# Layer 1's first deviation ahead of later gathers, idle products in the first tiles, another order for the maxima, and layer 0's clearing on GpSimd

## The chip, the core and the metric

## The reference

Two layers over x of 4 x 1024 rows of 256, with a context of 77 rows per batch. Each layer is cross-attention with 16 heads of 16 and then a feed-forward part: eight experts, two per row, in layer 0, and a low-rank one in layer 1.

```python
x = x + xattn0(_layernorm(x), ctx, ctx)       # Q = q@Wq ..., causal, softmax(Q K^T) V @ Wp
x = x + experts(_layernorm(x))                # router, top 2 of 8, gelu(x w1) w2, weighted sum
# layer 1's attention, the part that most of the change is in:
v = einsum('nlhd,ed->nlhe', v, Wv); k = einsum('nlhd,ed->nlhe', k, Wk); q = einsum('nlhd,ed->nlhe', q, Wq)
energy = einsum('nqhd,nkhd->nhqk', q, k)
attention = softmax(energy / sqrt(256), axis=-1)
x = x + (einsum('nhql,nlhd->nqhd', attention, v).reshape(N, Lq, 256) @ Wo.T + bo)
x = x + lowrank_ffn(_layernorm(x))            # gelu(x U1 V1 + b1) U2 V2 + b2
```

## The kernel before

The 4096 rows are 32 tiles of 128 (NT = 32), a group is four tiles. The order of every engine's instructions is written out by hand, as loops over steps k in each engine's block; `wait_ge` and `after` (the same, left out for values up to zero) are the waits. The stages follow one another with a barrier between them: preparation, `attend_first` (layer 0's attention), `route`, `experts`, `attend` (layer 1's attention) and `feed_forward`. Instructions of small helpers carry the helper's line.

**Layer 0's attention.** Step k turns the rows of tile k + 5 (L770), makes the queries of tile k + 4 (L778), which ScalarE scales into `qhi` (L828) and DVE into the low part (L899), and works on scores, exponentials and heads of earlier tiles. ScalarE copies the turned rows into `xT` (L866). GpSimd makes the reciprocal deviation `rstd` of tile k + 5 from DVE's variance (L656, L658), copies the high part into `qcat` twice (L631) and builds the block-diagonal keys `bd` (L623). Before the first step DVE clears `qcat` and `v_ps` (L892, L893), and ScalarE waits for `v_ok`, which the second of them sets, before all else.

**Layer 1's attention.** For tile f, two indirect DMAs on GpSimd's queue gather the experts' results `y1`, `y2` (L1583) while SP loads x; DVE adds them up and takes mean and variance (L1818 to L1828, the row work); GpSimd makes `rstd` and `shift` (L1600, L1603), and, one tile later, adds the bias `bo` to X (L1591); ScalarE norms the rows (L1757), PE turns them (L1705), ScalarE keeps the high f16 part (L1751) and DVE the low part (L1833). PE multiplies the high part with the keys, four products of four heads (`scores`, L1641), and DVE takes the maxima. For the first five tiles (EARLY) the four products go to the four banks of `sT_ps` and one instruction takes all maxima (L1844). For later tiles they share one bank, `s_ps`, so that each waits for the maximum before it (L1838). The maxima of a group are scaled by DVE (`mcat`, L1852), turned by PE (`maxima_transposed`, L1648) and copied by ScalarE to `mT` (L1784). Their place is `mT_ps`, in the bank `v_ps`, that also takes the values' products (L1679) and the turned heads (`heads_out`, L1632).

Then the scores are made again by key (`scores_by_key`, L1667) in four terms, the last of which subtracts the maxima; ScalarE takes exponentials (L1763), PE multiplies by the values, ScalarE copies out, PE turns the heads back, DVE divides by the sums (`heads`, L1859 and L1862), PE turns the result (L1690) and projects it (L1697) into the first half of `pr_bank`, and DVE adds it to X (`result`, L1868). Step k does this for quarter k, while its later part belongs to tile n = k - 5 and its earlier part to tile f = k + 5. Steps 5 to 26 have both and are called full here; a boundary is the passage from one group to the next. DVE's order in a full step is low part, heads, first and second maximum, row work of tile f + 2, third maximum, result, fourth maximum. PE's is heads, first scores, scores by key, second scores, and so on.

The experts' stage has idle products already, `awake` (L1328): products whose result nobody reads.

## Time and profile before

| | us |
|---|---|
| three runs, median (lowest to highest) | 1058.36 (1057.31 to 1061.56) |
| the profiled execution | 1060.01 |
| its span | 1058.0 |
| PE, DVE, ACT, POOL busy in it | 910.3, 621.1, 512.5, 423.3 |
| layer 0's attention begins, first work on PE | 36.4 |
| layer 1's attention, first gather to last result | 732.9 to 958.5 |

The profile records one execution. Its busy shares are means over stages with different limits, so they say little alone; the timeline gives, for each instruction or run of like ones, the start from the span's beginning, the time it took, and in brackets how long its engine had been idle and what ended that. A time "high" or "low" of the clock is the granted clock of 1.00 or 0.50.

### The profile page before, as it was taken

The page shows a single profiled execution, that of the slowest core. Times are in us where ns is not written, and L with a number is a line of the kernel's source. Part 1 is how long each engine was busy: PE and PEld are TensorE (multiplying, and loading weights), DVE is VectorE, ACT ScalarE, POOL GpSimd, SP SyncE. Part 2 cuts the span into 40 slices and gives each one's busy share as a digit, 9 for nine tenths or more (in the row PEclk, how much of TensorE's full clock was granted, in tenths as well). Part 3 has the DMA queues.
Part 4 walks back from the last instruction along what each step waited for, and adds up shares of the span by engine and source line. Part 5 has one row for each costly group of instructions (what it writes and reads, how often), then busy time and mean ns, then how long its engine had stood idle before and what let it go on. Part 6 is the DMA issues. An engine that isn't in the chain of part 4 may idle for free. (4 is left out here: it accounts for less than half of the span.)

```text
span 1058.0 us, 23850 instructions
## 1 busy us (share of the span) xinstructions
PE 910.3 (86%) x7874; PEld 627.0 (59%) x7874; DVE 621.1 (59%) x1484; ACT 512.5 (48%) x865; POOL 423.3 (40%) x592
## 2 busy tenths in 40 slices
PE   5799999997027999999999999995479888879996
PEld 3445656554016889898988989874124444445552
DVE  4567888876795444454444444322768888645561
ACT  1478888875311333323333333342266666645663
POOL 2377777762102423333221222212865665104451
PEclk9789999999557999999999999998568999999999
DMA  6323444334420111112111121112324222000212
GB/s 181 72 77 99 137 125 133 111 102 148 163 79 20 54 49 45 57 41 61 41 49 53 42 61 41 51 46 70 100 70 112 67 71 56 1 1 5 54 45 61
DMA packets 73727, 75.42 MB, mean 71 GB/s; under 512 B 22730, under 2 KB 66874, under 8 KB 73626
## 3 DMA queue, kind: packets, MB, share of 16 engines
q1 hardware_dynamic: 67146, 56.31, 17.9%
q0 software_dynamic: 6480, 17.70, 6.5%
q8 instruction: 71, 1.16, 0.5%
q14 instruction: 30, 0.25, 0.1%
HBM read 51.64 MB, written 22.34 MB: 70 GB/s over the span
## 5 line engine op out<-in xcount | busy, mean ns | idle before, releaser
L1496 DVE CAST hh_e<-h_e 128x512 f16<-128x512 f32 x128 | 59.4, 464 | 178.1 <-ACT h_e L1446 105.3
L1347 PE MATMUL up_ps<-xT_e,experts 128*128 128x256 f16 x512 | 139.6, 273 | 0.7 <-DVE xT_e L1488 0.6
L1361 PE MATMUL y_ps<-experts,hh_e 128*128 x512 | 139.6, 273 | 0.0
L1362 PE MATMUL y_ps<-experts,hh_e 128*128 x512 | 139.6, 273 | 0.0
L1348 PE MATMUL up_ps<-xT_e,experts 128*128 128x256 f16 x512 | 139.6, 273 | 0.0
L1363 PE MATMUL y_ps<-experts,hh_e 128*128 x512 | 139.6, 273 | 0.0
L1349 PE MATMUL up_ps<-xT_e,experts 128*128 128x256 f16 x512 | 139.6, 273 | 0.0
L1273 POOL COPY idx_e<-token 128x2 int32 (+2 forms) x39 | 22.5, 577 | 286.4 <-PE xT_ps_e L1322 237.0
L1446 ACT ACTIVATE h_e<-up_ps 128x512 f32<-128x512 f32 x128 | 76.4, 597 | 87.5 <-PE up_ps L1349 87.5
L1498 DVE TENSOR_TENSOR hh_e<-h_e,hh_e 128x512 f16<-128x512 f32 x128 | 88.6, 692 | 4.4
L1763 ACT ACTIVATE prob_a<-sT_ps_a 77x1024 f32<-77x1024 f32 x64 | 64.9, 1015 | 42.1 <-PE sT_ps_a L1667 42.1
L1276 POOL DMA_INDIRECT x_e<-xh_scratch,idx_e x71 | 69.5, 979 | 36.6 <-POOL idx_e L1273 26.9
L1583 POOL DMA_INDIRECT y_a<-y_scratch,slots_t x64 | 63.2, 987 | 36.9 <-POOLq L1266 21.6
L623 POOL TENSOR_TENSOR experts<-keys,blocks 128x616 f16<-128x616 f16 x64 | 76.5, 1216 | 0.0
L1439 ACT ACTIVATE xT_e<-xT_ps_e 128x512 f16<-128x512 f32 (+1 forms) x39 | 21.8, 558 | 100.2 <-PE xT_ps_e L1322 100.2
L820 ACT ACTIVATE experts<-sT_ps 77x1024 f32<-77x1024 f32 x64 | 65.1, 1018 | 8.4 <-PE sT_ps L692 5.4
L1838 DVE TENSOR_REDUCE nmax_a<-s_ps_a 128x4 f32<-128x308 f32 x108 | 51.2, 474 | 23.8 <-PE s_ps_a L1641 22.3
L2116 ACT ACTIVATE h_f<-h_ps_f,b_f 128x512 f32<-128x512 f32 x64 | 43.1, 687 | 30.2 <-PE h_ps_f L2058 30.2
L913 DVE TENSOR_REDUCE qcat<-s_ps 128x8 f16<-128x616 f32 x64 | 51.1, 798 | 8.7 <-PE s_ps L718 4.6
L1347 PEld LDWEIGHTS up_ps<-xT_e,experts 128*128 x512 | 50.1, 98 | 7.1 <-issue 1.2
L1362 PEld LDWEIGHTS y_ps<-experts,hh_e 128*128 128x128 f16 x512 | 50.1, 98 | 6.0
L1349 PEld LDWEIGHTS up_ps<-xT_e,experts 128*128 x512 | 50.1, 98 | 5.9
(328 smaller groups left out, 2115.0 us busy)
## 6 DMA issues: line engine op xcount, KB each, us to landing
experts<-in_L_ffn_w SPq DMA_DIRECT2D x22, 512.0 KB, 4.1
y_scratch<-y_e SPq DMA_DIRECT2D x32, 256.0 KB, 3.4
x<-in_x SPq DMA_DIRECT2D x32, 128.0 KB, 3.3
experts<-in_x SPq DMA_DIRECT2D x64, 64.0 KB, 2.5
x_scratch<-x SPq DMA_DIRECT2D x16, 256.0 KB, 2.5
xh_scratch<-xn SPq DMA_DIRECT2D x16, 256.0 KB, 2.8
w_r<-in_L_ffn_w SPq DMA_DIRECT2D x8, 512.0 KB, 4.3
x_a<-x_scratch SPq DMA_DIRECT2D x32, 128.0 KB, 2.6
```

The source lines that it names most:

```text
L623: nc.gpsimd.tensor_tensor(bd[:, f % 2, flat(i, 2), :, :], G["khi"][0][:, b, heads].rearrange("p (q k) -> p q k", q=2)[:, :, None, :] .broa ...
L820: nc.scalar.activation(prob[:, k % 2, qh, :, :], sT_ps[0:KEYS, :, :], ACT.Exp).then_inc(exp_ok, 1)
L1276: pool.indirect_dma_start(out=x[:, n, :], out_offset=None, in_=A["xh"], in_offset=bass.IndirectOffsetOnAxis(ap=idx[:, n:n + 1], axis=0)) \
L1347: mm(out, w[0], xT[0][:, c, 0:W_], start=c == 0, stop=False)
L1348: mm(out, w[0], xT[1][:, c, 0:W_], start=False, stop=False)
L1349: last = mm(out, w[1], xT[0][:, c, 0:W_], start=False, stop=c == DC - 1)
L1361: mm(out, a[0], w[0], start=m == 0, stop=False)
L1362: mm(out, a[0], w[1], start=False, stop=False)
L1363: last = mm(out, a[1], w[0], start=False, stop=m == 7)
L1446: nc.scalar.activation(h[:, q % 2, 0:2 * width(k)], up_ps[q][:, 0:2 * width(k)], ACT.Gelu, scale=1 / WSCALE).then_inc(gelu_ok, 1)
L1498: nc.vector.tensor_tensor(hh[1][own], h[own], hh[0][own], ALU.subtract).then_inc(hlo_ok, 1)
L1763: nc.scalar.activation(prob[:, k % 2, 2 * half:2 * half + 2, :], sT_ps[0:KEYS, 2 * half:2 * half + 2, :], ACT.Exp, scale=1.0 / 16).then_in ...
```

## The change

Layer 0: GpSimd clears `qcat` ahead of its steps, the low part of tile 0 waits for it (`qcat_ok`), and ScalarE's wait for `v_ok` goes. Six groups of six idle products are put between PE's first instructions. Layer 1: GpSimd's gather for tile f + 1 instead of f + 3 stands ahead of tile f's deviation, with two tiles gathered ahead of the loop and none in its first pass; the bias is added eight tiles later. PE does 52 idle products ahead of the first rows and two and six around each early tile's scores. `mT_ps` moves to the second half of `pr_bank`, with the waits that go with it. The second scores of a step are issued ahead of the last term of the scores by key, and DVE takes the first maximum between the reciprocal of the sums and the heads' product.

```diff
@@ attend_first, GpSimd
+                nc.gpsimd.memset(qcat[:, :, :, :], 0.0).then_inc(qcat_ok, 1)
+                pool.wait_ge(qcat_ok, 1)
                 for k in STEPS:
                     f = k + 3
                     if tile(k + 4):
-                        if k == -4:
-                            pool.wait_ge(v_ok, 1)
                         high_twice(k + 4)
@@ attend_first, PE
+                def awake(count):
+                    for i in range(count):
+                        mm(sT_ps[:, 0, 0:D], G["ident16"][:, :], G["khi"][0][:, 0, 0:D], start=True, stop=True)
                 for k in STEPS:
                     if tile(k + 4):
                         queries(k + 4, k)
+                    if k in (-4, -3):
+                        awake(6)
                     if tile(k + 3):
                         high_transposed(k + 3, k)
...
                         rows_transposed(k + 5, k)
+                    if k in (-5, -4, -3, -2):
+                        awake(6)
@@ attend_first, ACT and DVE
-                act.wait_ge(v_ok, 1)
-                nc.vector.memset(qcat[:, :, :, :], 0.0)
                 nc.vector.memset(v_ps[:, :], 0.0).then_inc(v_ok, 1)
...
+                    if f == 0:
+                        dve.wait_ge(qcat_ok, 1)
@@ attend
-        mT_ps = v_ps[:, 0:D].bitcast(F16)
+        mT_ps = pr_bank[:, D:2 * D].bitcast(F16)
@@ attend, GpSimd
-                for f in range(3):
+                LAG = 8
+                for f in range(2):
                     gather(f)
                 pool.wait_ge(bo_in, 16)
                 for f in range(NT):
-                    if f + 3 < NT:
-                        gather(f + 3)
+                    if f and f + 1 < NT:
+                        gather(f + 1)
...
-                    if f > 0:
-                        biased(f - 1)
-                biased(NT - 1)
+                    if f >= LAG:
+                        biased(f - LAG)
+                for f in range(NT - LAG, NT):
+                    biased(f)
@@ attend, PE
-                    pe.wait_ge(mT_ok, min(k // 4 + 1, GROUPS))
...
                 def maxima_transposed(g):
                     pe.wait_ge(mc_ok, g + 1)
-                    after(pe, oe_ok, 4 * g - 1)
+                    after(pe, mT_ok, g)
+                    after(pe, x3_ok, 4 * g - 5)
...
                 def scores_by_key(k):
-                    pe.wait_ge(mT_ok, g + 1)
                     for term in range(4):
+                        if term == 3:
+                            pe.wait_ge(mT_ok, g + 1)
+                            if tile(k + 5) and k + 5 not in EARLY:
+                                scores(k + 5, 1)
...
                 def projection(n):
+                    pe.wait_ge(mT_ok, min((n + 5) // 4 + 1, GROUPS))
...
+                awake(52)
                 for k in STEPS:
                     if f in EARLY:
+                        awake(2)
                         for i in range(4):
                             scores(f, i)
+                        awake(6)
...
                         scores_by_key(k)
-                    if late:
-                        scores(f, 1)
@@ attend, DVE
+                def sums(n):
+                    dve.wait_ge(o_done, n + 1)
+                    nc.vector.reciprocal(rec[:, n % 2, :], heads_bank(n)...[:, :, HD]).then_inc(rec_ok, 1)
...
                     if tile(n):
-                        heads(n)
+                        sums(n)
                     if late:
                         maximum(f, 0)
+                    if tile(n):
+                        heads(n)
+                    if late:
                         maximum(f, 1)
```

GpSimd's queue at the start of layer 1's attention, before (the gathers are the DMAs of y_a, `rstd_a` is the deviation, `X<-X,bo_a` the bias):

```order
L1583 DMA y_a<-y_scratch,slots_t 128x256 x6
L1583 DMA y_a<-y_scratch,slots_t 128x256 [waits bo_in_a]
L1583 DMA y_a<-y_scratch,slots_t 128x256
L1600 TENSOR_TENSOR rstd_a<-ve_a,neghalf 128x1 [waits var_ok_a]
L1603 TENSOR_SCALAR shift_a<-mv_a,rstd_a 128x1 [waits rstd_ok_a]
L1583 DMA y_a<-y_scratch,slots_t 128x256 [waits x2_ok_a]
L1583 DMA y_a<-y_scratch,slots_t 128x256
L1600 TENSOR_TENSOR rstd_a<-ve_a,neghalf 128x1 [waits var_ok_a]
L1603 TENSOR_SCALAR shift_a<-mv_a,rstd_a 128x1 [waits rstd_ok_a]
L1591 TENSOR_TENSOR X<-X,bo_a 128x256 [waits xh_ok_a]
```

and now:

```order
L1592 DMA y_a<-y_scratch,slots_t 128x256 x4
L1610 TENSOR_TENSOR rstd_a<-ve_a,neghalf 128x1 [waits var_ok_a,bo_in_a]
L1613 TENSOR_SCALAR shift_a<-mv_a,rstd_a 128x1 [waits rstd_ok_a]
L1592 DMA y_a<-y_scratch,slots_t 128x256 x2
L1610 TENSOR_TENSOR rstd_a<-ve_a,neghalf 128x1 [waits var_ok_a]
L1613 TENSOR_SCALAR shift_a<-mv_a,rstd_a 128x1 [waits rstd_ok_a]
```

Four gathers stand ahead of the first deviation instead of eight, and the bias has left these rows.

PE's queue at a group's boundary in layer 1's attention, with the beginning of the next step, before (`s_ps_a` are scores, `sT_ps_a` the scores by key, `v_ps_a<-const,oTu_a` the heads, `mcat_a` the maxima):

```order
L1641 MATMUL s_ps_a<-keys,xhi_a 128x308 [waits max_ok_a]
L1648 MATMUL v_ps_a<-ident,mcat_a 128x128 [waits oe_ok_a,mc_ok_a]
L1648 MATMUL v_ps_a<-ident,mcat_a 128x128 x3
L1632 MATMUL v_ps_a<-const,oTu_a 128x128 [waits mT_ok_a,oe_ok_a]
L1632 MATMUL v_ps_a<-const,oTu_a 128x128 x3
L1641 MATMUL s_ps_a<-keys,xhi_a 128x308 [waits max_ok_a,hi_ok_a]
L1667 MATMUL sT_ps_a<-xhi_a,keys 77x512 [waits exp_ok_a,lo_ok_a,mT_ok_a]
L1667 MATMUL sT_ps_a<-xhi_a,keys 77x512 x3
L1667 MATMUL sT_ps_a<-xlo_a,keys 77x512 x4
L1667 MATMUL sT_ps_a<-xhi_a,keys 77x512 x4
L1667 MATMUL sT_ps_a<-mT_a,mrows 77x512 x4
L1641 MATMUL s_ps_a<-keys,xhi_a 128x308 [waits max_ok_a]
```

and now:

```order
L1651 MATMUL s_ps_a<-keys,xhi_a 128x308 [waits max_ok_a]
L1660 MATMUL pr_ps_a<-ident,mcat_a 128x128 [waits x3_ok_a,mT_ok_a,mc_ok_a]
L1660 MATMUL pr_ps_a<-ident,mcat_a 128x128 x3
L1642 MATMUL v_ps_a<-const,oTu_a 128x128 [waits oe_ok_a]
L1642 MATMUL v_ps_a<-const,oTu_a 128x128 x3
L1651 MATMUL s_ps_a<-keys,xhi_a 128x308 [waits max_ok_a,hi_ok_a]
L1682 MATMUL sT_ps_a<-xhi_a,keys 77x512 [waits exp_ok_a,lo_ok_a]
L1682 MATMUL sT_ps_a<-xhi_a,keys 77x512 x3
L1682 MATMUL sT_ps_a<-xlo_a,keys 77x512 x4
L1682 MATMUL sT_ps_a<-xhi_a,keys 77x512 x4
L1651 MATMUL s_ps_a<-keys,xhi_a 128x308 [waits max_ok_a,mT_ok_a]
L1682 MATMUL sT_ps_a<-mT_a,mrows 77x512 x4
```

The wait for the eviction has moved from the heads to the last term, a wait for DVE's result has come ahead of the turned maxima, and the second scores have changed places with the last term.

DVE's queue in a full step, before (`nmax_a` the maxima, `o_a` the heads' product, `xa_a` the row work's first instruction):

```order
L1859 RECIPROCAL rec_a<-v_ps_a 128x16 [waits o_done_a]
L1862 TENSOR_TENSOR o_a<-v_ps_a,rec_a 128x256 [waits oT_done_a,rec_ok_a]
L1838 TENSOR_REDUCE nmax_a<-s_ps_a 128x4 [waits s_done_a] x2
L1818 SCALAR_TENSOR_TENSOR xa_a<-y_a,cw_t,x_a 128x256 [waits x_in1_a,y_in1_a]
L1821 SCALAR_TENSOR_TENSOR X<-y_a,cw_t,xa_a 128x256 [waits xa_ok_a]
```

and now:

```order
L1880 RECIPROCAL rec_a<-v_ps_a 128x16 [waits o_done_a]
L1860 TENSOR_REDUCE nmax_a<-s_ps_a 128x4 [waits s_done_a]
L1887 TENSOR_TENSOR o_a<-v_ps_a,rec_a 128x256 [waits oT_done_a,rec_ok_a]
L1860 TENSOR_REDUCE nmax_a<-s_ps_a 128x4 [waits s_done_a]
L1840 SCALAR_TENSOR_TENSOR xa_a<-y_a,cw_t,x_a 128x256 [waits x_in1_a,y_in1_a]
```

The heads' product stands between the first two maxima.

## Rows read from the trace of the kernel before

**Rows 1.** Stretches: us, busy (instructions) by engine, PEclk (granted clock), DMA share, GB/s

```profile
740.00:760.00 20.00, 7.59 (x24) 2.88 (x24) 13.41 (x28) 4.47 (x9) 16.92 (x25) 0.50 0.36 102
...
784.00:788.00 4.00, 4.00 (x26) 0.85 (x25) 2.29 (x7) 1.02 (x2) 2.04 (x3) 0.50 0.24 68
...
820.00:860.00 40.00, 34.63 (x291) 17.69 (x290) 34.05 (x95) 27.32 (x45) 25.55 (x38) 1.00 0.25 71
```

**Rows 2.** Timeline, layer 0's start and one memset before it: start, us, engine, instruction

```profile
8.39 0.95 POOL L259 MEMSET experts<- 128x1024 f16 x1
...
36.82 1.76 DVE L892 MEMSET qcat<- 128x2048 uint32 x1 [0.78 <-PEq L223]
...
39.21 0.38 ACT L866 ACTIVATE experts<-t_ps 128x256 f32<-128x256 f32 x1 [3.42 <-DVE v_ps L893]
...
40.09 0.57 POOL L658 TENSOR_TENSOR rstd<-ve,neghalf 128x1 f32<-128x1 f32 x1
...
41.81 0.47 ACT L828 ACTIVATE experts<-q_ps,rstd 128x256 f16<-128x256 f32 x1 [1.27 <-PE q_ps L778]
...
54.50 0.47 ACT L828 ACTIVATE experts<-q_ps,rstd 128x256 f16<-128x256 f32 x1 [1.97 <-POOL rstd L658]
```

**Rows 3.** Timeline, layer 1's first tiles, and the gathers' own view, last row

```profile
734.16 0.95 POOL L1583 DMA_INDIRECT y_a<-y_scratch,slots_t  x1 [0.30 <-issue]
...
737.66 0.48 DVE L1818 SCALAR_TENSOR_TENSOR xa_a<-y_a,cw_t,x_a 128x256 f32<-128x256 f32 x1 [4.47 <-DMA y_a<-y_scratch,slots_t]
...
739.38 0.15 DVE L1828 TENSOR_SCALAR ve_a<-mv_a 128x1 f32<-128x1 f32 x1
...
742.73 0.59 POOL L1600 TENSOR_TENSOR rstd_a<-ve_a,neghalf 128x1 f32<-128x1 f32 x1
...
746.17 0.58 POOL L1600 TENSOR_TENSOR rstd_a<-ve_a,neghalf 128x1 f32<-128x1 f32 x1
...
746.87 1.44 DVE L1844 TENSOR_REDUCE nmax_a<-sT_ps_a 128x16 f32<-128x1232 f32 x1 [0.92 <-PE sT_ps_a L1641]
...
747.08 0.72 POOL L1591 TENSOR_TENSOR X<-X,bo_a 128x256 f32<-128x256 f32 x1
...
747.96 1.03 POOL L1583 DMA_INDIRECT y_a<-y_scratch,slots_t  x1 [0.17 <-issue]
...
750.28 0.58 POOL L1600 TENSOR_TENSOR rstd_a<-ve_a,neghalf 128x1 f32<-128x1 f32 x1
...
DMA to landing us min/median/max: 2.7/2.8/4.4
```

**Rows 4.** Timeline, a full step, and the result of a group earlier or later

```profile
841.88 0.41 DVE L1868 TENSOR_TENSOR X<-pr_ps_a,X 128x256 f32<-128x256 f32 x1
...
843.71 0.47 DVE L1838 TENSOR_REDUCE nmax_a<-s_ps_a 128x4 f32<-128x308 f32 x1
...
844.24 0.30 PE L1641 MATMUL s_ps_a<-keys,xhi_a 128*128 128x308 f16 x1
...
844.58 0.48 DVE L1838 TENSOR_REDUCE nmax_a<-s_ps_a 128x4 f32<-128x308 f32 x1 [0.40 <-PE s_ps_a L1641]
...
847.14 0.41 DVE L1868 TENSOR_TENSOR X<-pr_ps_a,X 128x256 f32<-128x256 f32 x1
...
864.33 0.41 DVE L1868 TENSOR_TENSOR X<-pr_ps_a,X 128x256 f32<-128x256 f32 x1
```

**Rows 5.** Waits from 804 to 910 us: who for whom, us, times, longest

```profile
DVE nmax_a L1838 <- PE s_ps_a L1641: 7.6, 19, 0.4
...
DVE rec_a L1859 <- PE v_ps_a L1632: 4.1, 5, 0.8
```

**Rows 6.** Timeline of PE: the experts' idle products

```profile
326.69 5.30 PE L1328 MATMUL up_ps<-experts,ident 128*128 128x256 f16 x24 [3.69 <-PEq L1061]
```

**Rows 7.** Timeline, exponentials of the first and the sixth step

```profile
769.61 1.93 ACT L1763 ACTIVATE prob_a<-sT_ps_a 77x1024 f32<-77x1024 f32 x2
...
799.30 1.02 ACT L1763 ACTIVATE prob_a<-sT_ps_a 77x1024 f32<-77x1024 f32 x1 [2.07 <-PE sT_ps_a L1667]
```

17 lines of the change are left out of this document (11 added, 6 removed).

## The prediction

> **What bounds the kernel now.** I read the busy shares by stage first [rows 1]. Layer 1's attention, from 732 us on, is the stage that most of the change touches. From 740 to 760 us TensorE (PE) is busy 7.59 of 20 us, at a granted clock of 0.50 (1.2 of 2.4 GHz), and GpSimd 16.92 of 20 us. So its first tiles hang on GpSimd; the timelines show that the steps after them hang on PE and DVE in turn.
>
> *Layer 0's start* [rows 2]: DVE clears qcat (1.76 us) and then v_ps; ScalarE waits 3.42 us for that and makes xT of tile 0 only at 39.21; the queries follow, and qhi of tile 0 comes at 41.81. Its reciprocal deviation was ready at 40.09 + 0.57 = 40.66. Three tiles on, the same ScalarE instruction waits for GpSimd instead (1.97 us at 54.50), and GpSimd's own loop sets the pace.
>
> *Layer 1's start* [rows 3]: tile 0's variance is ready at 739.38 + 0.15 = 739.53 (its data came at 737.66), but GpSimd has eight indirect gathers of about 1.25 us each ahead of its deviation, which starts at 742.73. Then GpSimd is full: two gathers, deviation, shift and bias addition make 4.11 us per tile (746.17 to 750.28).
>
> *A full step at the high clock* [rows 4], one of about 20: the first maximum (843.71) ends at 844.18; TensorE can only then overwrite s_ps (844.24), and the second maximum starts at 844.58. DVE waits 0.40 us, and this wait is there 19 times between 804 and 910 us, 7.6 us in all [rows 5]. DVE has no other wait of that size in a plain step. The step is 5.26 us (the result's starts, 841.88 and 847.14). *At a group's boundary* PE waits for ScalarE to evict the maxima from v_ps, and DVE then up to 0.8 us for the heads behind it: 4.1 us in five boundaries [rows 5]. Four steps with one boundary take 864.33 - 841.88 = 22.45 us [rows 4]. That is 4 x 5.26 = 21.04 and 1.41 more: about 0.5 us for DVE's scaling of the maxima, an instruction as long as a maximum's 0.47, and 0.9 for the boundary.
>
> **The change part by part.** All is summed against the profiled execution, 1060.01 us (span 1058.0); it lies 1.65 us above the median of the three runs, 1058.36.
>
> *1. Layer 0's start.* v_ok no longer holds ScalarE: xT of tile 0 can start at about 36.9, and its queries end near 38.6. But qcat is now cleared on GpSimd, ahead of tile 0's deviation on the same queue, as 4096 elements of two bytes. GpSimd's memset of 1024 such took 0.95 us [rows 2]: four times that is 3.8 us, and a little less, 3.5, since an instruction's fixed part is paid once. From 36.8 that is 40.3, then about 0.4 us to the deviation and 0.57 for it: it is ready at 41.3, 0.65 us later than now, and qhi of tile 0 starts at about 41.35 instead of 41.81: **-0.45 us**. What was the late input (the queries) is early, and the deviation is late next. The 36 idle products lie in these steps too; 24 such products took 5.30 us at the low clock [rows 6], 0.21 us each with 0.2 for the last one's latency, and at the high clock it would be 0.11. Twelve of them stand between one tile's queries and the next tile's in the third step: 2.6 us low, 1.3 high. At the high clock a tile's own queries would take about 1 us less. With GpSimd next in line (54.50) most of either is hidden. Bounds: -1.5 us (one tile's queries gained) to +2.2 (2.6 us paid, 0.45 kept).
>
> The Trainium skill says in "VectorE: DVE Perf Modes", section on zero memsets as uint32, that a memset costs one cycle per element whatever the type, so that clearing by four bytes halves it. It speaks against this move: with GpSimd's 1.2 GHz (the Trainium skill, "GPSIMD Engine Reference", Specifications) 4096 elements would be 3.4 us, an estimate, against the 2048 words that DVE cleared. GpSimd's own row agrees with it, and term 1 would be -0.55 us by it.
>
> *2. Layer 1's first deviation.* Four gathers stand ahead of it instead of eight. They end at about 737.6, so it waits only for the variance and starts at 739.6 instead of 742.73: **-3.1 us** for tile 0. Tile 1's follows the next two gathers, at 743.0 instead of 746.17, the same.
>
> *3. The first tiles after it.* The bias addition (0.72 us, 0.88 with its gap: 747.08 to 747.96) leaves GpSimd's loop for eight tiles: 4.11 - 0.88 = 3.23 us. DVE is next: low part, early maxima (1.44 us) and row work need 0.4 + 1.4 + 1.9 = 3.7 us (the row work from 737.66 to 739.53), and a gather now runs only one tile ahead, landing 2.8 us after its issue in the median and about 3.5 at the first (734.16 to 737.66) [rows 3]. Walking the chain tile by tile gives 3.7 to 4.0 us, seven tiles of 0.1 to 0.4 less, minus a hold-up at tile 2 of up to 0.4. I take **-1.2 us** (bounds -0.6 to -1.9). The bias additions return from tile 8 on in GpSimd's idle time (1 to 2 us a step) and the last eight run at its end, where nothing is due soon.
>
> *4. 92 idle products in layer 1.* Fifty-two stand ahead of the first transposes. The 24 from 326.69 on ran at the low clock to the end [rows 6]; the 52 go on for twice as long. If half of the 52 run at 0.21 and half at 0.11 us, they end near 740.6, and the first transposes are due at 741.3: nothing. All at the low clock, they end at 743.3: +2.0. The eight per tile (1.7 us low, 0.9 high) fit into PE's idle time (12.4 of 20 us [rows 1], five tiles: 2.5 us each). Gain: the five steps from the first exponentials (769.61) to the sixth step's (799.30) take 29.7 us now [rows 7], 5.9 each, mostly at 0.50. At the high clock a maximum, its turn through PE and the next maximum are 0.87 us apart (843.71 to 844.58), 0.93 to 0.97 with what lies between; three of these, 0.4 and the row work of 1.8 make 5.0 us a step, and with one scaling of the maxima 25.5 us: -4.2. At the low clock PE is full, 6.6 us a step at most; the second scores go ahead of a quarter of the score work, 0.4 us earlier: 6.2 a step, 31 us: +1.3. No products stand in these steps, and from 784 us on the clock was at 0.50 although PE was busy 4.00 of 4 us [rows 1]. So I take mostly low: **-1.2 us** (bounds -4.2 to +2.8, the latter with one step with heads at the low clock, 1.5 us more).
>
> *5. Maxima reordered.* In a full step DVE now does low part, reciprocal, first maximum, head product, second maximum; PE issues the second scores ahead of the last term. With [rows 4]: the first maximum can start at 843.37 and ends at 843.84; scores at 843.95, 0.30 us; second maximum at 844.30 instead of 844.58: 0.28 saved of the 0.40. But two more chains then lie at about 5.0 us: PE's own (0.28 us of its small gaps, about 0.45 a step, go) and the projection, that waits on exponentials which now start after the second scores. I take 0.23: 21 steps (the sixth to the 26th, as the loops count them) x 0.23 = **-4.8 us** (0 to -8.4).
>
> *6. Maxima through pr_bank.* PE need no longer wait for the eviction before the heads. But the transposes now wait for the result that DVE reads from that bank (847.14 + 0.41, behind the third maximum), and then stand ahead of the heads: about 0.2 us of wait is left of 0.9, so 0.7 at each of six boundaries with heads: **-4.2 us** (-2 to -5.5).
>
> Sum: -0.45 - 3.1 - 1.2 - 1.2 - 4.8 - 4.2 = **-14.95 us**, or 1045.1 for the profiled execution and **1043 us** for a median (1058.36 - 14.95 = 1043.4). The last stage starts earlier by the whole of it, since it waits for this one only.
>
> **The rivals.** (a) *The clock stays high through the first steps.* The sum's term 4 becomes -4.2: 1040 us. For it: steps with heads, little different in kind, run at it. Against: 784 to 788 us [rows 1]. [...] (b) *The reordering moves the wait.* The exponentials come later behind the second scores, PE's queue with them, and the step stays at 5.26: without term 5, 1048 us. (c) *The products are paid at the low clock*: term 1 at +2.2, term 4 at +2.8: 1043.4 + 2.65 + 4.0 = 1050. (d) *Slower: the clock stays low in the steps with heads.* A step at the low clock takes some 6 us without heads; heads, their transposes and the projection add about 2 us there: 8 against 5.0, 3 us more a step. It decides from the fifth such step on (15 us), from the seventh by over 0.5%; ten make 1043 + 30 = 1073 us. Against it: with heads the clock is at 1.00 and PE busy 34.63 of 40 us from 820 on [rows 1], and shorter waits leave PE busier, not idler. (e) *The first deviation is not what holds the first tiles*, since gathers landing late take its place: term 2 halved and term 3 at zero, 1046 us, within the forecast's range.
>
> **How the numbers follow.** Forecast with (e) 0.55; (a) 0.18; (b) 0.12; (c) 0.12; (d) 0.03. The range from 1035 (a with terms 5 and 6 at their better bounds, in part) to 1051 (c) leaves about 2 in 10 out. A measurement of this kernel tells 0.5%, 5.3 us, from no change: faster by more needs less than 1053, which all but (d) and the end of (c) give: 0.92; within 0.5%: 0.05; slower: 0.03.
>
> **What would show it.** Tile 0's deviation at 3 us before its old place, from the stage's start; early maxima 3.7 to 4.0 us apart; the wait of 0.40 us ahead of the second maximum below 0.15 and full steps of 5.0 us; four steps with a boundary in about 20.8 us; no wait of PE for the eviction. In layer 0 qhi of tile 0 within half a microsecond of now, behind GpSimd's clearing of 3.5 us. The granted clock from 741 to 800 us tells (a) from the forecast. The prediction is wrong if full steps stay at 5.26 us, or if the products stand ahead of transposes that are ready.

## The result, and the profile after

| | us |
|---|---|
| before, seven runs | 1059.04 (1054.92 to 1061.56) |
| changed, seven runs | 1051.73 (1046.83 to 1058.75) |
| ratio, 95% interval | 0.9937 (0.991 to 0.9964) |
| changed, the profiled execution (span) | 1047.91 (1045.8) |
| changed, all 19 executions, later ones included | 1049.65 (1040.53 to 1059.79) |

The change gains 7.3 us in the first seven runs and 9.4 over all its executions; the forecast had 15 to 16. The changed kernel's 19 executions lie 19 us apart, those of the kernel before 4 to 9 in each group of runs. A ratio leaves out executions over 1.5% above the fastest of their kernel, which here touches one only, the 1059.79 of e5.

Among the first seven runs the time goes with the mean granted clock: 1046.8 and 1047.9 us at 0.945, 1057.6 and 1058.8 at 0.932 and 0.933. The profiled execution is the second fastest of them and 3.8 us below their median, so its trace shows more gain than the median does.

Where the 12.2 us between the two profiled executions lie, with two later profiles of the same changed kernel (e5, e17) beside them:

| stretch | before | changed | e5 | e17 | forecast of the difference |
|---|---|---|---|---|---|
| layer 0: DVE's first clearing to `qhi` of tile 0 | 4.99 | 4.42 | 4.42 | 4.43 | -0.45 |
| layer 0: DVE's first clearing to the router's logits | 242.67 | 240.21 | 240.28 | 248.60 | the same -0.45 |
| layer 1: `mcat` cleared to the copy-out of quarter 0 | 44.25 | 39.86 | 39.79 | 39.84 | -4.3 (terms 2, 3) |
| copy-outs 0 to 5 (steps 0 to 4) | 29.58 | 31.25 | 29.99 | 25.34 | -1.2 (term 4) |
| copy-outs 5 to 26 (full steps) | 116.17 | 110.96 | 111.02 | 109.75 | -8.3 (term 5, five boundaries of term 6) |
| copy-out 26 to the last result | 36.14 | 34.60 | 35.96 | 34.61 | -0.7 (the sixth boundary) |

Each interval runs from start to start; DVE's first clearing is that of `qcat` in the kernel before (36.82) and that of `v_ps` in the changed one (36.48). The rows add up to 11.9 us; the other 0.3 lie elsewhere.

The timeline of the changed kernel at both starts (answers to [rows 2], [rows 3] and, for idle products, [rows 6]):

```profile
36.29 3.52 POOL L642 MEMSET qcat<- 128x4096 f16 x1 [21.65 <-POOLq L223]
36.48 0.48 DVE L900 MEMSET v_ps<- 128x512 f32 x1 [0.47 <-PEq L223]
40.24 0.57 POOL L658 TENSOR_TENSOR rstd<-ve,neghalf 128x1 f32<-128x1 f32 x1
40.90 0.47 ACT L837 ACTIVATE experts<-q_ps,rstd 128x256 f16<-128x256 f32 x1 [2.80 <-POOL rstd L658]
...
729.28 5.84 PE L1727 MATMUL pr_ps_a<-keys,ident 128*128 128x256 f16 x52 [2.59 <-PEq L1275]
735.07 0.48 DVE L1840 SCALAR_TENSOR_TENSOR xa_a<-y_a,cw_t,x_a 128x256 f32<-128x256 f32 x1 [4.85 <-DMA y_a<-y_scratch,slots_t]
737.11 0.68 POOL L1610 TENSOR_TENSOR rstd_a<-ve_a,neghalf 128x1 f32<-128x1 f32 x1 [2.48 <-DVE ve_a L1850]
741.34 1.44 DVE L1866 TENSOR_REDUCE nmax_a<-sT_ps_a 128x16 f32<-128x1232 f32 x1 [0.92 <-PE sT_ps_a L1651]
744.81 1.43 DVE L1866 TENSOR_REDUCE nmax_a<-sT_ps_a 128x16 f32<-128x1232 f32 x1
```

GpSimd's clearing takes 3.52 us (estimate 3.5), and `qhi` of tile 0 now waits 2.80 us for the deviation behind it. In layer 1 the deviation starts 737.11 - 729.36 = 7.75 us after `mcat` is cleared, where it was 742.73 - 732.33 = 10.40; it waits for DVE's variance now, not for the later gathers ahead of it in its queue. That variance follows tile 0's own data, which landed 735.07 - 729.36 = 5.71 us after the clearing and not 737.66 - 732.33 = 5.33: this later landing takes 0.4 of the 3.1 us that were forecast. The next early maximum follows in 3.47 us. The 52 products took 5.84 us, 0.11 each: all at the high clock, and over (735.12) as DVE's first row work began (735.07).

A full step and the waits from 804 to 910 us (answers to [rows 4] and [rows 5]):

```profile
839.39 0.42 DVE L1893 TENSOR_TENSOR X<-pr_ps_a,X 128x256 f32<-128x256 f32 x1 [0.21 <-PE pr_ps_a L1713]
...
840.69 0.48 DVE L1860 TENSOR_REDUCE nmax_a<-s_ps_a 128x4 f32<-128x308 f32 x1
841.09 0.41 DVE L1887 TENSOR_TENSOR o_a<-v_ps_a,rec_a 128x256 f32<-128x256 f32 x1
841.70 0.48 DVE L1860 TENSOR_REDUCE nmax_a<-s_ps_a 128x4 f32<-128x308 f32 x1 [0.20 <-PE s_ps_a L1651]
...
844.56 0.42 DVE L1893 TENSOR_TENSOR X<-pr_ps_a,X 128x256 f32<-128x256 f32 x1 [0.21 <-PE pr_ps_a L1713]
...
860.88 0.42 DVE L1893 TENSOR_TENSOR X<-pr_ps_a,X 128x256 f32<-128x256 f32 x1 [0.21 <-PE pr_ps_a L1713]
```

```profile
DVE nmax_a L1860 <- PE s_ps_a L1651: 6.5, 20, 1.5
DVE X L1893 <- PE pr_ps_a L1713: 5.7, 20, 0.6
...
DVE rec_a L1880 <- PE v_ps_a L1642: 1.4, 5, 0.3
```

DVE's wait ahead of the second maximum is 0.20 us, half of the 0.40 before. A new wait of 0.21 us stands ahead of the result, for the projection. The boundary's wait ahead of the reciprocal fell from 4.1 to 1.4 us. The step from 839.39 to 844.56 is 5.17 us, and four steps with a boundary take 860.88 - 839.39 = 21.49 (5.26 and 22.45 before).

ScalarE's copy-outs of the quarters 0, 5 and 26, before and then changed, mark the stretches of the table:

```profile
776.58 0.60 ACT L1769 ACTIVATE oTu_a<-v_ps_a 128x512 f32<-128x512 f32 x1 [1.06 <-PE v_ps_a L1679]
806.16 0.60 ACT L1769 ACTIVATE oTu_a<-v_ps_a 128x512 f32<-128x512 f32 x1 [0.21 <-PE v_ps_a L1679]
922.33 0.60 ACT L1769 ACTIVATE oTu_a<-v_ps_a 128x512 f32<-128x512 f32 x1 [0.25 <-PE v_ps_a L1679]
```

```profile
769.22 0.60 ACT L1791 ACTIVATE oTu_a<-v_ps_a 128x512 f32<-128x512 f32 x1 [0.85 <-PE v_ps_a L1694]
775.91 0.60 ACT L1791 ACTIVATE oTu_a<-v_ps_a 128x512 f32<-128x512 f32 x1 [0.85 <-PE v_ps_a L1694]
...
800.47 0.60 ACT L1791 ACTIVATE oTu_a<-v_ps_a 128x512 f32<-128x512 f32 x1
...
911.43 0.60 ACT L1791 ACTIVATE oTu_a<-v_ps_a 128x512 f32<-128x512 f32 x1 [0.30 <-PE v_ps_a L1694]
```

The dense steps 0 to 4 gave 1.7 us back: the first three take 6.69 us each at the low clock (769.22 to 775.91 for one).

Two stretches, columns as in [rows 1], 766 to 792 us for the dense steps:

```profile
740.00:760.00 20.00, 13.08 (x81) 7.88 (x85) 17.08 (x37) 5.51 (x11) 14.68 (x21) 0.84 0.36 102
766.00:792.00 26.00, 23.85 (x128) 6.83 (x124) 15.95 (x43) 13.71 (x21) 13.96 (x20) 0.50 0.31 80
```

The clock was at 0.84 in the early tiles (0.50 before) and at 0.50 in the dense steps, with PE busy 23.85 of 26 us.

Three questions follow. What are the idle products worth, and do they make the executions differ? Why do terms 5 and 6 bring 5.2 us instead of 8.3 in the full steps? What sets the clock in steps 0 to 4?

### The profile page after: what moved, and what is told of

Its sections match the earlier page's. It is cut to its first block and busy times, and to the rows that moved or that the text cites. A ratio compares the mean times of both kernels' runs of the same rounds, so it can differ in the third digit from the quotient of the medians.

```text
span 1045.8 us, 24107 instructions
## 1 busy us (share of the span) xinstructions
PE 920.9 (88%) x8002; PEld 636.3 (61%) x8002; DVE 612.4 (59%) x1483; ACT 510.1 (49%) x865; POOL 426.8 (41%) x593
## 5 line engine op out<-in xcount | busy, mean ns | idle before, releaser
L1505 DVE CAST hh_e<-h_e 128x512 f16<-128x512 f32 x128 | 55.3, 432 | 183.1 <-ACT h_e L1455 118.8
```

## Experiments

Every kernel computes all of the reference. "Changed" is the kernel after the change.

| run | kernel | median (lowest to highest), runs | ratio to before, interval |
|---|---|---|---|
| e1 | changed, no products in layer 1 | 1046.58 (1044.22 to 1050.58), 5 | 0.9871 (0.9845 to 0.9897) |
| e2 | changed, no products in layer 0 | 1046.95 (1042.76 to 1049.82), 6 | 0.9888 (0.9863 to 0.9913) |
| e3 | changed, order of maxima as before | 1050.08 (1047.84 to 1057.09), 7 | 0.9922 (0.9894 to 0.995) |
| e4 | before, order of maxima alone | 1055.77 (1047.94 to 1060.52), 12 | 0.997 (0.9946 to 0.9993) |
| e5 | changed again | 1047.79 (1040.53 to 1059.79), 6 | 0.9886 (0.9847 to 0.9925) |
| e6 | changed, no products at all | 1047.05 (1046.37 to 1048.09), 6 | 0.9891 (0.9869 to 0.9913) |
| e7 | before, gathers alone | 1056.63 (1052.55 to 1059.91), 12 | 0.9975 (0.9957 to 0.9994) |
| e8 | changed, more products in steps 0 to 4 | 1044.68 (1042.19 to 1057.69), 6 | 0.9899 (0.9854 to 0.9944) |
| e9 | e8 without layer 0's products | 1041.98 (1039.29 to 1044.52), 5 | 0.9842 (0.9817 to 0.9868) |
| e10 | products in steps 0 to 4 alone | 1041.29 (1038.75 to 1045.67), 6 | 0.9841 (0.9816 to 0.9866) |
| e11 | before, products alone | 1057.49 (1055.51 to 1062.27), 12 | 0.9999 (0.9979 to 1.0019) |
| e12 | before, maxima's bank alone | 1055.60 (1051.15 to 1058.10), 12 | 0.9962 (0.9944 to 0.998) |
| e13 | e10 with layer 0's products | 1042.86 (1041.61 to 1045.41), 5 | 0.9856 (0.9837 to 0.9874) |
| e14 | e10 again | 1045.15 (1044.47 to 1047.24), 4 | 0.9879 (0.9861 to 0.9897) |
| e15 | e10, second scores between halves | 1045.57 (1043.27 to 1046.99), 4 | 0.9875 (0.9855 to 0.9895) |
| e16 | before, products in steps 0 to 4 | 1064.06 (1060.39 to 1065.75), 6 | 1.005 (1.0033 to 1.0067) |
| e17 | changed, third time | 1049.56 (1044.46 to 1050.77), 6 | 0.9902 (0.9875 to 0.993) |
| e18 | e10, third time | 1040.41 (1039.01 to 1043.88), 5 | 0.9838 (0.9812 to 0.9865) |

### The products taken away: e1, e2, e6, and alone: e11

e1 takes this out:

```diff
-                awake(52)
...
-                        awake(2)
...
-                        awake(6)
```

> The changed kernel without the idle products of layer 1 (52, and eight per early tile). The changed kernel ran at 1051.7 us in the median, spread over 12 us, where the one before spread over 6.6. Theory 1: the products give a high clock from about 742 to 756 us and nothing after; the early tiles go by DVE and GpSimd, so without the products the time is 0 to 1.5 us longer (1052 to 1053) and the spread stays. Theory 2: the products are what makes the executions differ, since work done ahead of the dense steps moves the low stretch of the clock into them: without them the median falls to 1047 to 1049 and the spread to 7 us or less, and the first five dense steps take 29.7 us or less instead of 31.0.

e2 takes out layer 0's two:

```diff
-                    if k in (-4, -3):
-                        awake(6)
...
-                    if k in (-5, -4, -3, -2):
-                        awake(6)
```

> The changed kernel without the 36 idle products of layer 0. In its profile the clock was high from 46 us on where it had been low to 56 us before, and the route stage began 2.8 us earlier. Theory 1: all of that but the earlier deviation (0.9 us) comes from the products: without them the median is 1.5 to 2 us longer, about 1053.5, and the clock is low from 40 to 55 us again. Theory 2: it comes from ScalarE's earlier start and GpSimd's loop, and the products are idle cost: the median stays within 0.5 us of 1051.7, and the route stage still begins within 0.5 us of 276.7.

e6 takes out all four.

> The changed kernel without any of its idle products, in layer 0 as in layer 1. Theory 1 (products neither gain nor cost): 1047 us like each half, groups of 21.1 us, the first five dense steps 29.5 to 31.3. Theory 2 (each half's products cost about 5 us in the median): 1042 to 1044. Theory 3 (the products gain, and the two kernels without half of them drew well): 1050 or more, with the clock low from 40 to 55 us.

e11 is the kernel before with the same four places filled.

> The kernel before with only the idle products of both layers, placed as in the change. Theory 1 (they gain 0.4 us in layer 0 and nothing in layer 1, and widen the spread): a median of 1057 to 1060 us, executions from 1050 to 1066. Theory 2 (they gain what the forecast gave them, 1 to 3 us): 1056 to 1058, spread 6 us. In either, the clock is high through the early tiles of layer 1, where GpSimd sets the pace, so that no time is gained there.

Without the products of either layer the time does not rise. It is 1046.6, 1047.0 and 1047.1 us in e1, e2 and e6, against 1049.65 over the changed kernel's 19 executions, and e6's six executions lie within 1.7 us. Beside e6, though, the changed kernel itself (e5) ran at 1047.8 with a ratio of 0.9886, where e6 has 0.9891: side by side there is no difference, so that the products cost anything in the median is not shown. In the kernel before the products alone bring nothing (0.9999, give or take 2 us; its median is 1.5 us lower), and its executions lie no further apart there. So the change's gain comes from its other parts. Theory 1 of e1 (up to 1.5 us longer) was wrong; of its theory 2 the lower median held, but e1's first five dense steps took 31.23 us, so the products do not move the low clock into those. Both theories of e2 were wrong (1053.5, and 1051.7 with the next stage at 276.7): it ran at 1047.0, and its logits came at 275.18 us. For e6, theory 1 had the median and the dense steps (31.25) right, but its groups of four steps took 21.5 us and not 21.1. For e11, the median fits both theories, the spread theory 2.

### Where a long execution can lose its time: e17, with e5

e5 and e17 are the changed kernel unaltered.

> The changed kernel itself again, on the chip and beside the kernels of this call. Theory 1 (its executions differ by where the clock is low, and the seven before were a wide draw): a median of 1048 to 1051 us, a profile whose groups of four steps take 21.1 us like those of the two kernels without products (they took 21.5 in most of its first profile). Theory 2 (the products cost): 1051 to 1053 again, 4 us or more above the kernel without any, and groups of 21.5 us.

> The changed kernel a third time. Theory 1 (products ahead of the dense steps in both layers leave room for a long low stretch in layer 0's or layer 1's dense steps in some executions): a median of 1048 to 1052, and one execution or more above 1055. Theory 2 (the calls differ, not the kernels): within 2 us of e18.

The medians were 1047.8 and 1049.6 us, near theory 1's in both; but e5's profile has groups of four steps at 21.5 us (theory 1: 21.1), and e5 had an execution at 1059.79, e17 none above 1050.8 (its theory 1: one above 1055). e17's profile shows where a long one can lose time. Layer 0's stretches 60 to 90 us of the changed kernel, of e17, of e18 and of the kernel before (columns as in [rows 1]):

```profile
60.00:75.00 15.00, 13.53 (x146) 6.88 (x144) 10.62 (x22) 14.01 (x22) 11.84 (x16) 1.00 0.15 43
75.00:90.00 15.00, 13.66 (x154) 7.88 (x151) 8.97 (x22) 13.52 (x23) 10.88 (x16) 1.00 0.46 137
```

```profile
60.00:75.00 15.00, 15.00 (x104) 7.54 (x103) 6.37 (x14) 9.48 (x14) 7.43 (x10) 0.50 0.20 49
75.00:90.00 15.00, 14.78 (x125) 6.97 (x127) 7.50 (x17) 11.54 (x18) 8.98 (x12) 0.67 0.29 89
```

```profile
60.00:75.00 15.00, 13.17 (x152) 7.29 (x152) 10.65 (x22) 14.18 (x23) 11.95 (x15) 1.00 0.16 42
```

```profile
60.00:75.00 15.00, 14.11 (x135) 7.09 (x134) 8.63 (x19) 11.87 (x19) 11.06 (x15) 0.77 0.13 39
```

In e17 PE ran at 0.50 while it was busy 15.00 of 15 us, and did 104 matmuls instead of 146. The router's logits, first of the changed kernel and then of e17, with e17's clearing of `v_ps` ahead:

```profile
276.69 0.49 DVE L1132 TENSOR_TENSOR logits<-logits,lx 128x128 f32<-128x128 f32 x2 [1.53 <-PEq L537]
```

```profile
38.29 0.48 DVE L900 MEMSET v_ps<- 128x512 f32 x1 [0.47 <-PEq L223]
...
286.89 0.49 DVE L1132 TENSOR_TENSOR logits<-logits,lx 128x128 f32<-128x128 f32 x2 [1.52 <-PEq L537]
```

From the clearing they come 276.69 - 36.48 = 240.21 and 286.89 - 38.29 = 248.60 us later: layer 0 took 8.4 us longer with this low stretch. Over all profiles of kernels with GpSimd's clearing the interval is, with layer 0's products, 240.2, 240.3, 240.5, 241.6, 242.3, 243.9 and 248.6 (changed, e5, e8, e13, e1, e3, e17; the clock fell below 1.00 between 60 and 90 us in the last four), and without them 239.2 to 239.7 six times and 242.1 once (e15, 0.77 from 60 to 75). The means are 242.5 and 239.9. Two things lie in that difference of 2.6 us.

The first is there at the high clock too. With the clock at 1.00 from 60 us on, the interval is 240.2 to 240.5 with the products (changed, e5, e8) and 239.2 to 239.7 without (six profiles): they cost 0.8 us, although they bring the early steps, which GpSimd paces, 0.3 to 0.4 us forward (the clock is at 0.97 from 45 to 60 us, 0.61 in e18 without them). In the kernel before it is 241.3 (e11) against 240.4 and 239.9 (e7, e16).

The second is the low stretch between 60 and 90 us, and it comes without layer 0's products as well: in the kernel before itself (0.77 from 60 to 75 us, above), in e4 (0.88), in e12 (0.94) and in e15 (0.77). That makes four of twelve profiles without the products and four of eight with them; the two at 0.50 (e3, e17) both have them. Whether the products bring the low stretch or make it longer is therefore not shown. It also means that the 2.5 us by which the first profile gains in layer 0 are the low stretch in the profile before: e7 and e16, with the old clearing and the clock at 1.00 there, need 240.4 and 239.9 us, not 242.67, and the changed kernel needs 240.2.

e17's dense steps were fast by luck, as the next part shows; an execution with its layer 0 and the first profile's dense steps would be 1049.5 + 31.25 - 25.34 = 1055.4 us, close to the three highest (1057.6 to 1059.8). That those are such executions is inferred from their mean granted clock (0.931 to 0.933, where the profiled ones had 0.945); none of them has a profile.

### The dense steps 0 to 4: e8, e9, e10, e14, e18, e16

e8 adds, behind the last term:

```diff
                     if 0 <= k < QUARTERS:
                         scores_by_key(k)
+                    if 0 <= k < 5:
+                        awake(6)
```

> The changed kernel with six more idle products in each of the steps 0 to 4, behind the last term, where the clock was low from 766 to 793 us. Theory 1 (PE's gaps there keep the clock low): the clock is high from the second of these steps on, and the five steps take 27 us instead of 31.2: 1048. Theory 2 (PE is full at the low clock and the clock comes back by another cause): each product is paid, 6 x 0.21 = 1.26 us a step, 37 us for the five: 1057.

e9 is e8 without layer 0's products, e10 has these products alone.

> The changed kernel without layer 0's idle products, with layer 1's and six more in each of the steps 0 to 4. Theory 1 (the dense steps stay at the high clock when PE's gaps are filled, and layer 0's products bring nothing but a low stretch that falls later): the five steps take 26.6 to 27 us in the profile as in the kernel with all products, the median is 1042.5 to 1044, and no execution lies above 1052. Theory 2 (the far executions come from layer 1's products): the median is about 1044.7 and one in six lies above 1054.

> The changed kernel with no idle products but the six in each of the steps 0 to 4. Theory 1 (products there lift the clock by themselves): the clock, low up to quarter 0, is high from the first or second of these steps on, the five take 27 to 28.5 us instead of 31.25, the median falls from 1047 to 1043.5 or less, and the spread stays at 2 to 3 us. Theory 2 (the clock has to be high before, and at the low clock PE is full, so products are paid): 31.25 + 5 x 1.26 = 37.5 us and a median of 1053.

e14 and e18 repeat e10; e16 puts the products of steps 0 to 4 alone into the kernel before.

> The kernel of e10 again, beside the other three. Both theories: 1040 to 1043 us, steps 0 to 5 in 26.0 us, groups of 21.1 us or with three steps longer by 0.4 us.

> The kernel of e10 and e14 a third time, beside the changed kernel. Theory 1: 1041 to 1045.5 us, 5 us or more below e17, spread 3 to 7 us. Theory 2: within 2 us of e17.

> The kernel before with only six idle products in each of the steps 0 to 4. Theory 1 (the clock stays or turns high once PE's gaps there are filled, whatever the order around): steps 0 to 5 take 26.3 us instead of 29.6, 1055.5 in the median. Theory 2 (the new order of scores is needed for it, since PE's waits at group boundaries and for the maxima are larger here): 29 to 34 us and 1058 to 1063.

The stretches 770 to 790 us of e6, e10 and e16, in this order:

```profile
770.00:780.00 10.00, 8.89 (x52) 2.37 (x56) 5.85 (x16) 4.03 (x8) 5.46 (x7) 0.50 0.21 62
780.00:790.00 10.00, 9.47 (x49) 3.03 (x42) 6.05 (x17) 6.34 (x10) 5.01 (x8) 0.50 0.31 90
```

```profile
770.00:780.00 10.00, 7.95 (x72) 3.19 (x64) 7.44 (x21) 6.23 (x10) 6.44 (x10) 1.00 0.30 81
780.00:790.00 10.00, 9.30 (x80) 4.46 (x79) 8.12 (x23) 7.08 (x13) 6.45 (x10) 1.00 0.75 165
```

```profile
770.00:780.00 10.00, 8.82 (x53) 2.98 (x53) 4.94 (x13) 3.88 (x6) 5.41 (x8) 0.50 0.15 41
```

With 30 products in these steps the clock is high from the first of them on, and copy-outs 0 to 5 take 26.0 us in e9, e10 and e18, 26.6 in e8 and e14, 27.0 in e15 and 28.0 in e13, whose second step takes 6.83 us (both are described below; e6: 31.25). e10, e14 and e18 are 1041.3, 1045.2 and 1040.4 us, and e18 stands 9 us below the changed kernel beside it (e17), the largest gain of the study; e14 fell short of its expectation by 2 us. Theory 1 held for e8, e9, e10 and e18, with times at or below its own, though e10's executions lie 7 us apart and not 2 to 3. e8, which has layer 0's products too, had two executions at 1051.5 and 1057.7 among six. Theory 2, by which PE is full there and each product is paid, is wrong: six take 0.83 us at the high clock (the row is e10's), and the step falls by 1.4 us with them in it (6.69 to 5.30).

```profile
770.89 0.83 PE L1723 MATMUL pr_ps_a<-keys,ident 128*128 128x256 f16 x6
```

But e16, for which theory 2 held, shows that it isn't the products alone: in the kernel before the clock was at 0.50 from 770 to 780 with them, copy-outs 0 to 5 took 30.4 us, and the time rose by 0.5%. Of the 3.1 us that its profile loses from the clearing of `mcat` to copy-out 5, 2.3 lie ahead of copy-out 0 (46.50 us, 44.25 before), where step 0's products stand. And e17 and e4 had the high clock with no product in these steps. Copy-outs 0 and 5 of e17, and copy-out 0 of e4, whose copy-out 5 stands in the next part:

```profile
778.20 0.60 ACT L1791 ACTIVATE oTu_a<-v_ps_a 128x512 f32<-128x512 f32 x1 [0.56 <-PE v_ps_a L1694]
...
803.54 0.60 ACT L1791 ACTIVATE oTu_a<-v_ps_a 128x512 f32<-128x512 f32 x1
```

```profile
778.28 0.60 ACT L1770 ACTIVATE oTu_a<-v_ps_a 128x512 f32<-128x512 f32 x1 [0.85 <-PE v_ps_a L1682]
```

That is 25.34 us, 5.07 a step, in e17, and 26.33 in e4 (clock 0.81 from 780 to 790 us and 1.00 from then on). So the clock was high for most of these steps in all seven profiles that have the products there together with the new order, and in two of the twelve profiles that have no products there. What decides at the end of the early tiles which way the clock goes is open.

### The maxima: e3, e4, e12, e15

e3 puts scores and maxima of the changed kernel back in the old order, e4 puts only the new order into the kernel before, e12 only the new bank and its waits.

```diff
@@ e3 (e4 is the reverse, on the kernel before)
-                        if term == 3:
-                            if tile(k + 5) and k + 5 not in EARLY:
-                                scores(k + 5, 1)
...
+                    if late:
+                        scores(f, 1)
@@ e12
-        mT_ps = v_ps[:, 0:D].bitcast(F16)
+        mT_ps = pr_bank[:, D:2 * D].bitcast(F16)
```

> The changed kernel with the second scores behind the last term again and both maxima behind the heads' product, as before the change; the maxima's bank stays the new one. Theory 1: the reordering is worth what full steps show between the two traces, less the boundaries: 0.1 us in a plain step and 0.4 in one with scaling, so about 3 us: 1054.7, with steps of 5.26 to 5.3 and the wait of 0.4 us ahead of the second maximum back. Theory 2: it is worth the 0.23 us a step of the forecast, and the bank almost nothing: 1056.5. Theory 3: it is worth nothing, since the projection's wait takes its place: 1051.7, and the boundaries alone carry the 5.4 us of the full steps.

> The kernel before with only the reordering of scores and maxima (second scores ahead of the last term, first maximum between reciprocal and heads' product); its maxima still go through the heads' bank. Theory 1: about 3 us less than the kernel before, 1056; the wait ahead of the second maximum falls from 0.40 to about 0.2 us and a new one of about 0.25 ahead of the result appears. Theory 2: 4.8 us less, 1054, steps of 5.03. Theory 3: no difference, 1059, since the wait for the evicted maxima, which then stands ahead of heads with the second scores later behind them, grows by what is gained.

> The kernel before with only the maxima's bank changed and the waits that go with it. Theory 1: four steps with a boundary take 21.76 us as in the changed kernel with the old order, 0.69 us a boundary less than 22.45, five or six boundaries: 3.5 to 4.2 us less, 1055. Theory 2: the wait at a boundary only goes from the heads to the turned maxima, 22.2 us and 1058.

Copy-outs 5 and 26 of e4 and of e12, with waits of e4:

```profile
804.61 0.60 ACT L1770 ACTIVATE oTu_a<-v_ps_a 128x512 f32<-128x512 f32 x1
...
916.68 0.60 ACT L1770 ACTIVATE oTu_a<-v_ps_a 128x512 f32<-128x512 f32 x1 [0.30 <-PE v_ps_a L1682]
```

```profile
805.23 0.60 ACT L1770 ACTIVATE oTu_a<-v_ps_a 128x512 f32<-128x512 f32 x1 [0.21 <-PE v_ps_a L1679]
...
918.12 0.60 ACT L1770 ACTIVATE oTu_a<-v_ps_a 128x512 f32<-128x512 f32 x1 [0.25 <-PE v_ps_a L1679]
```

```profile
DVE X L1872 <- PE pr_ps_a L1700: 4.4, 20, 0.4
...
DVE rec_a L1859 <- PE v_ps_a L1632: 4.1, 5, 0.8
```

The stretch is 116.17 us before, 112.07 with the order alone (-4.1), 112.89 with the bank alone (-3.3), 112.71 in e3 (-3.5, the bank with the rest of the change and the old order) and 109.75 with both in e17 (-6.4; e1, e2, e9, e10 and e18 have it within 0.03). So each part works, by 4.1 against a forecast of 4.8 and 3.3 against 3.5 (five of its six boundaries lie in the stretch), and together they lose another 1.0. In e4's copy-outs the plain step is 5.17 us instead of 5.26, the step with scaling 5.24 instead of 5.75, the boundary's 5.98 instead of 6.17: 0.88 in four steps, and most of it not where the forecast had it. By the stretch, e3 should lie 1.8 (first profile) to 3.0 us (e17) above the changed kernel, as its theory 1 has it; its median, 1050.1, lies within 0.5 of it, as theory 3 has it. That is less than its executions (9 us apart, with layer 0's clock at 0.50 from 60 to 75 us in its profile) can tell. Theory 1 of e4 and of e12 held. The profile of e4 gains another 3.3 us in the dense steps, where its clock was high; how many of its other executions had that is not known (they lie 13 us apart).

e15 asks what holds the step at 5.17 us:

```diff
-                        if term == 3:
-                            ...
-                                scores(k + 5, 1)
                         for r in range(4):
+                            if (term, r) == (3, 2) and tile(k + 5) and k + 5 not in EARLY:
+                                scores(k + 5, 1)
```

> The kernel of e10 with the second scores between the two halves of the last term, so that the first half's exponentials can start about 0.2 us earlier and the second scores come 0.2 us later. Theory 1 (the projection behind the exponentials bounds the step, and the result's wait of 0.21 us is its mark): that wait falls below 0.1 us, the plain step goes from 5.17 to about 5.05, four steps from 21.1 to 20.6, and the time by 2 to 3 us to 1039. Theory 2 (VectorE's second maximum bounds it): the wait ahead of it grows from 0.15 to 0.35, the step becomes 5.3, 1044. Theory 3 (the third scores and PE's queue bound it): unchanged, 1041.3.

Waits from 804 to 910 us, e10 and then e15:

```profile
DVE X L1888 <- PE pr_ps_a L1709: 9.7, 21, 2.8
DVE nmax_a L1855 <- PE s_ps_a L1647: 5.8, 16, 1.5
```

```profile
ACT oTu_a L1786 <- PE v_ps_a L1690: 10.6, 20, 0.7
DVE nmax_a L1855 <- PE s_ps_a L1647: 10.6, 21, 1.4
DVE X L1888 <- PE pr_ps_a L1709: 3.3, 3, 2.6
```

(Each has one or two long waits from the end of the full steps in it.) The result's wait is gone, 3 instead of 21 times, and DVE's for the maxima rose from 5.8 to 10.6 us: the plain step became 5.32 us, the four steps 21.55. Theory 2 held in the trace; in the medians e15 is only 0.4 us above e14 beside it (1045.57 and 1045.15). At 5.17 us the two chains, second maximum and projection, are balanced, and what one is given the other loses.

### Layer 0's products again, and the gathers alone: e13, e7

> The kernel of e10 (idle products only in the steps 0 to 4) with the 36 idle products of layer 0 added again. Theory 1 (they bring tile 1's queries 0.35 us forward and let the clock fall again between 60 and 75 us, in the dense steps of layer 0, in some executions for long): a median of 1042 to 1046 us and at least one execution more than 6 us above it. Theory 2 (the far executions have another cause): as e10, 1041 to 1042, spread 7 us.

e13 came out 2.3 us below e14 beside it, with none of its five executions far, which speaks for theory 2. Its profile has the low stretch (0.77 from 60 to 75 us, 241.62 us to the logits against e14's 239.51), but layer 0 began at 35.67 us and not at 37.99, as in e14. So layer 0's products cost 0.8 us in the profiles at the high clock, and no difference of medians confirms or denies it.

e7 is the kernel before with only the new order of gathers and bias additions.

> The kernel before with only the new order of layer 1's gathers and bias additions. Theory 1: the first exponentials come 3.5 to 4.5 us earlier from the stage's start, as in the changed kernel (the copy-out of quarter 0 at 40.4 us instead of 44.3), and the steps after them are untouched: 1055. Theory 2: the dense steps, reached earlier, stay longer at the low clock and give it back: 29.6 us become 31 to 33, and the median is 1057 to 1059.

Its copy-out of quarter 0 comes at 40.28 us (44.25 before), and 1056.63 is 2.4 us below before: copy-outs 0 to 5 took 30.71 us instead of 29.58, so that part of the 4.0 us was given back in the low clock, as its theory 2 has it in a weak form.

## Why the prediction was wrong, point by point

**Direction and mechanism** were right for five of six terms, and the size was not: 1043 with a lower end of 1035 and an upper of 1051, against 1051.73 (1049.65 over all). The steps that failed are terms 4, 5 and 6: of the 14.95 us of the sum, 2.9 are lost in the dense steps and 3.5 in the full steps and the boundaries, as told below. The first profile makes up for part of it in stretches where the sum had little (2.0 us in layer 0, 1.2 at the end), so it gains 12.1. Why the median gains less than the profile is known only as far as the granted clock goes, which is lower in the longer executions. Of the parts alone, e7, e4, e12 and e11 gain 2.4, 3.1, 3.4 and 1.5 us in their medians. With 0.6 for the clearing, which was never run alone, that is 11.0 us, against the 9.4 of the changed kernel; each of these is uncertain by about 2 us, so it is no test of how they add up.

**Term 1, layer 0** (-0.45): the wait worked as forecast (`qhi` of tile 0 0.57 us earlier, behind 3.52 us of clearing). The estimate of 3.4 us, worked out from the Trainium skill ("VectorE: DVE Perf Modes", section on zero memsets as uint32, and "GPSIMD Engine Reference", Specifications), agrees with the 3.52 of the trace. By the profiles without a low stretch the clearing is worth 0.7 us at the logits (means of 240.15 and 239.49) and the products take 0.8 of it back, inside the bounds. What the bounds leave out is the low stretch from 60 to 90 us, which the profile before had too and which makes layer 0 1 to 8 us longer.

**Terms 2 and 3, gathers** (-4.3): -4.4 at the copy-out of quarter 0, -2.7 of it at the first deviation (forecast -3.1) and the rest through gaps of 3.45 to 4.66 us between early maxima. Right. The first deviation waits for the variance, so rival (e) did not occur as it stands, but late data took a little: 0.4 us at the first tile, and tile 3's maximum came 1.10 us late behind a gather.

**Term 4, clock** (-1.2): the clock was high through the early tiles (0.84 from 740 to 760 us) and low in the dense steps, as in the forecast, but a low step takes 6.69 us and not 6.2. The step that failed is "the second scores go ahead of a quarter of the score work, 0.4 us earlier": 6.69 us is the 6.6 "at most" of the forecast with nothing taken off. e3, the changed kernel with the old order, shows what the order does there. Its copy-outs 1 and 2:

```profile
777.73 0.60 ACT L1791 ACTIVATE oTu_a<-v_ps_a 128x512 f32<-128x512 f32 x1 [1.22 <-PE v_ps_a L1692]
784.27 0.60 ACT L1791 ACTIVATE oTu_a<-v_ps_a 128x512 f32<-128x512 f32 x1 [1.22 <-PE v_ps_a L1692]
```

That is 6.54 us a step at 0.50, and e11, with the old order, has a step of 6.54 too: so the new order costs 0.15 us a step at the low clock, where the forecast had it gain 0.4. Nor is PE full in such a step (5.89 of 6.70 us busy from 769.2 us on); what holds the step is open. The term was +1.7. In another execution of the same kernel, e17, rival (a) occurred, with 5.07 us a step against its 5.0. The Trainium skill says in "TensorE: Matmul & The Clock Gate", Part 1, that activity releases the low clock. e10's dense steps, where products were added, fit that; e17's layer 0 does not, with PE busy 15.00 of 15 us at 0.50, and neither does e16, with 8.82 of 10 us at 0.50 and the products in place.

**Term 5, order** (-4.8): -4.1 alone, -3.0 on top of the bank (112.71 to 109.75). Alone it is 0.20 us a step, near the 0.23, on the bank 0.14; the plain step, for which the 0.23 was worked out, fell by 0.09, from 5.26 to 5.17. The prediction named the projection's chain "at about 5.0 us" and took it as not binding; it binds at 5.17: DVE waits for it 20 times between 804 and 910 us, and e15, which takes that wait away, brings the other back. Rival (b), by which the wait only moves, was half true.

**Term 6, bank** (-4.2): -3.3 alone (e12), 0.66 at each of the five boundaries between copy-outs 5 and 26. The price of 0.7 was right there. At the sixth, behind copy-out 26, the step went from 5.17 to 4.84 us, 0.33. Of the 8.3 us of both terms in the full steps 5.2 came: 0.9 is size, 1.0 the overlap of the two, which the sum left out, and 1.2 the two rhythms told of in the last section, whose cause is open.

**The last part** gave 1.54 us, 1.2 more than the sixth boundary's 0.33; in e5, with the same code, it gave 0.2 in all.

**The range.** It was built from one profiled execution on each side. A spread between executions of one kernel by the clock lies in none of its cases, and (c), the case of its upper end, had the products paid at a fixed price. A term for a low stretch that comes in some executions (8.4 us in e17's layer 0) would have held the result, which lies 0.7 us outside.

## What to carry to other kernels

Look for the stretch that PE paces and that runs at the low level, and try idle products in that: 30 in five steps took the ratio from 0.9891 to 0.9841, 0.9879 and 0.9838. Leave alone the stretches that another engine paces, where 128 products brought nothing. Measure it in the kernel at hand, for the same 30 in another order of instructions made it 0.5% slower. Before giving an engine an operand earlier, walk the chain that the same move makes later: here two waits of 0.2 us took the place of one of 0.4. And take several profiles of a kernel whose executions differ, and of the one it is compared with: the changed kernel's was among its best, and the one before had a low stretch in layer 0 that others of it do not have.
